# A later order on TensorE in the self-attention loop, and two products that nothing reads behind each of the last five maxima pairs

## The chip, the cores and the metric

One NeuronCore of one Trainium2 chip runs the whole network in one launch. The metric is the device time of that launch in microseconds, as a median of several executions. Five engines work side by side and meet at semaphores: TensorE (PE, with its weight loads shown as PEld), VectorE (DVE), ScalarE (ACT), GpSimd (POOL), and SyncE (SP), which here only issues transfers. Products land in PSUM, eight banks of 128 x 512 fp32.

## The reference

Four layers over x of shape (4, 512, 128), each an attention and a feed-forward part. The change touches the last feed-forward part alone, a transformer block with 16 heads of 8 columns and a mixture of eight experts, of which each token takes one. Cut to what matters:

```
hn = layernorm(x, ln1_g, ln1_b)                      # 4 batches of 512 tokens
q, k, v = hn @ wq + bq, hn @ wk + bk, hn @ wv + bv   # 16 heads of 8
scores = q @ k.T / sqrt(8)                           # 512 x 512 for each head
attn = softmax(scores)                               # with the maximum of each row
x = x + (attn @ v) @ wo + bo
hn2 = layernorm(x, ln2_g, ln2_b)
idx = argmax(hn2 @ gate_w + gate_b)                  # one expert a token
x = x + (relu(hn2 @ w1[idx] + b1[idx]) @ w2[idx] + b2[idx])
```

## The kernel before, in words

`order` (line 2290) writes out the order of all work, and each engine's function runs it once with its own generators, so each engine gets its own instruction stream in one common order. `weave` takes generators with a list of times each (the n-th piece of a generator has the n-th time, or n divided by a number) and always lets the piece with the smallest time go next; on a tie the generator that was given first goes. The times are places in an order and no durations.

**The self-attention loop.** 16 steps, numbered s; a step is one batch (s // 4) and one group of four heads (g = s % 4). Each turn i of the loop (line 2343) works on four steps at once:

- `first(i)`: two pieces of two 128x128 by 128x512 products with selector matrices `SELm` (kept in `RR`, columns 6144 to 8191), which spread queries and keys of four heads over strips of 32 partitions. ScalarE copies them into `QS` and `KS`, which are `QB` and `KB` in a profile.
- `second(i - 1)`: eight pieces, the maxima pairs. TensorE multiplies 32-row queries with 32-row keys into two neighbouring banks (out of banks 0 to 3), and VectorE takes the row maxima of both (line 1825, 128x1024). A ninth piece on TensorE (line 886) transposes the 16 columns of maxima; ScalarE copies them (line 1290), and SyncE sends them by four small transfers (line 2134) into the spare rows of `QS`.
- `third(i - 2)`: waits for these four transfers, then sixteen pieces, one 32-row product each into banks 4, 5 and 6 in turn. The maximum is subtracted inside the product through the spare row. ScalarE follows with an exponential of 128x512 (line 1299). In a profile these products are `PS<-QB,KB`; those of the maxima pairs are `PS<-KB,QB`.
- `fourth(i - 3)`: four pieces of four 128-row products with 32 columns of values each, one for each strip of the array, all into bank 7; fp32 makes two instructions of each, so a piece shows as eight. ScalarE then copies bank 7 to `OT` (line 1307, semaphore `ots`).

Beside them run, in some turns only: `self_norms` (turns 2, 6, 10: the layer norm, values and projections of the next batch; TensorE's transposes are line 837), `tail4` (turns 7, 11, 15: the output of a batch is transposed, normalised and projected, lines 611 and 619), `route3` (turns 8, 12, 16: second layer norm, gate, rank of each token; the sums are line 1855) and `place3` (turn 14). A turn that has none of these is called plain below.

Banks 0 to 3 are given out in pairs where a pair is wanted and singly elsewhere (`Banks.take`, `take_pair`); a bank that was given out waits for its last reader.

Of the kernel before, what the change touches and what calls it, by code (L numbers as in the profile page):

```python
# [164 lines left out]
def program(nc, A, out):  # L165
    with ExitStack() as ctx:
# [292 lines left out]
        def tensor(e, w):  # L459
# [457 lines left out]
            def route3(b):  # L917
# [20 lines left out]
                yield from idle(6)  # L938
# [29 lines left out]
            def place3(g):  # L968
# [4 lines left out]
                yield from idle(14)  # L973
# [73 lines left out]
            order(norm, ahead, front, back, tail, prepare, route, capacity, l2_prepare, self_norms, first, second, third, fourth, tail4,  # L1047
# [3 lines left out]
        def scalar(e, w):  # L1051
# [234 lines left out]
            def second(s):  # L1286
                yield from idle(8)
                w.wait_ge(*mxT.at("s", s))
# [24 lines left out]
            def route3(b):  # L1313
# [5 lines left out]
                yield from idle(10)  # L1319
# [52 lines left out]
            order(norm, ahead, front, back, tail, prepare, route, capacity, l2_prepare, self_norms, first, second, third, fourth, tail4,  # L1372
# [3 lines left out]
        def vector(e, w):  # L1376
# [441 lines left out]
            def second(s):  # L1818
                w.wait_ge(*(mxT.at("s", s - 2) if s >= 2 else scored.at(23, 3, 3)))
                for t in range(4):  # L1820
                    for p2 in range(2):
# [4 lines left out]
                        yield  # L1826
                yield
# [10 lines left out]
            def route3(b):  # L1838
# [19 lines left out]
                yield  # L1858
# [145 lines left out]
            order(norm, ahead, front, back, tail, prepare, route, capacity, l2_prepare, self_norms, first, second, third, fourth, tail4,  # L2004
# [3 lines left out]
        def gpsimd(e, w):  # L2008
# [59 lines left out]
            def route3(b):  # L2068
                yield from layernorm(2, ("r3", b))
                yield from idle(13)  # L2070
# [36 lines left out]
            order(norm, nothing, nothing, nothing, nothing, nothing, route, nothing, nothing, self_norms, nothing, nothing, nothing, nothing, tail4,  # L2107
# [3 lines left out]
        def sync(e, w):  # L2111
# [18 lines left out]
            def second(s):  # L2130
                yield from idle(8)
# [128 lines left out]
            order(nothing, nothing, front, nothing, nothing, nothing, nothing, capacity, nothing, nothing, nothing, second, nothing, nothing,  # L2260
# [29 lines left out]
        def order(norm, ahead, front, back, tail, prepare, route, capacity, l2_prepare, self_norms, first, second, third, fourth, tail4,  # L2290
# [52 lines left out]
            for i in range(19):  # L2343
# [16 lines left out]
                if i in (8, 12, 16):  # L2360
                    streams.append((route3((i - 8) // 4), 26))
# [129 lines left out]
```

## Time and profile before

| what | us |
|---|---|
| median of the runs (3) | 1321.78 |
| lowest and highest | 1306.33, 1324.37 |
| the profiled execution: its own time | 1307.19 |
| its span, first to last instruction | 1305.4 |
| of the span: from the first to the last transpose of maxima | 834.3 to 1171.1 |
| mean granted TensorE clock, whole span | 0.818 of full speed |

The span is one execution. PE busy counts time in which any product is under way, whatever its height. PEclk is the clock that TensorE was granted: 0.50 stands for 1.2 GHz and 1.00 for 2.4 GHz all through a stretch, and a value between them is a mix of both. "Idle before" names what released an engine after it had waited.

### The profile page before, as it was taken

Reading aid. Unit: us, or ns where it says so; the run is one execution under the profiler, and the core shown is the slowest. Engines: PE = TensorE matmul, PEld = TensorE weight load, DVE = VectorE, ACT = ScalarE, POOL = GpSimd, SP = SyncE. Lnnn points to the kernel's source line nnn. Section 1 sums busy time; section 2 is a strip of 40 time slices with the busy share of each in tenths; the row PEclk is TensorE's granted clock in tenths of the full one; section 3 lists DMA queues with packets and bytes.
Section 4 is the critical chain, followed back from the end, with each engine's and each line's share of the span. In section 5 each row is a group of like instructions: output and inputs, shape, how many; then the busy total and the mean of one; then the engine's idle time right before and its main releaser. Section 6 shows DMA issues by size and latency. Waiting matters only on the chain.

```text
span 1305.4 us, 14785 instructions
## 1 busy us (share of the span) xinstructions
PE 1063.3 (81%) x5560; PEld 567.7 (43%) x5560; DVE 635.1 (49%) x1651; ACT 438.3 (34%) x842; POOL 139.6 (11%) x136
## 2 busy tenths in 40 slices
PE   4788999999976773866988887699888889778984
PEld 2344576665523432653653333333333343334653
DVE  4345656555544442337434434755564554652532
ACT  2334333232232220112313233255454454444431
POOL 1000000000011012025211001100100100200222
PEclk7789999999987775986889789676686875768987
DMA  9500000000210001121010000000000000001122
GB/s 294 162 1 1 1 1 1 1 1 1 88 42 4 4 6 35 41 56 21 2 38 1 1 1 1 1 1 1 1 1 1 1 1 1 17 1 31 41 62 71
DMA packets 31359, 33.73 MB, mean 26 GB/s; under 512 B 4053, under 2 KB 22893, under 8 KB 31160
## 3 DMA queue, kind: packets, MB, share of 16 engines
q1 hardware_dynamic: 29240, 28.99, 7.2%
q0 software_dynamic: 2048, 3.79, 1.1%
q8 instruction: 45, 0.74, 0.2%
q14 instruction: 26, 0.21, 0.1%
HBM read 23.31 MB, written 9.70 MB: 25 GB/s over the span
## 4 chain that ended last, share of the span: by engine, by line
PE 70%; DVE 18%; issue 5%; ACT 4%; POOL 2%; DMA 1%; SPq 0%; POOLq 0%; DVEq 0%; ACTq 0%
PE PS L177 63%; DVE KB L1825 4%; DVE KB L1494 3%; PE PS L611 3%; DVE Ht L1396 1%; POOL OT L2030 1%; DVE OT L1535 1%; PE PS L1005 1%; DVE st L1383 1%; POOL ve L2013 1%; DVE CX L1535 1%; PE PS L619 1%; PE PS L521 1%; ACT CX L1299 1%; ACT PT L1177 0%
## 5 line engine op out<-in xcount | busy, mean ns | idle before, releaser
L1825 DVE TENSOR_REDUCE KB<-PS 128x2 fp32r<-128x1024 f32 x128 | 153.6, 1222 | 125.6 <-PE PS L177 125.5
L1177 ACT ACTIVATE PT<-PS 77x512 f32<-77x512 f32 x192 | 98.2, 591 | 158.7 <-PE PS L177 158.7
L177 PE MATMUL PS<-CX 32*77 32x512 f32 (+2 forms) x896 | 128.2, 582 | 18.6 <-DVE OT L1535 7.6
L177 PE MATMUL PS<-HT,RA 128*128 128x512 f32 x288 | 132.0, 601 | 0.0
L2013 POOL TENSOR_TENSOR ve<-ve,nh 128x4 f32<-128x4 f32 x40 | 41.5, 1037 | 694.4 <-DVE ve L1391 694.4
L177 PE MATMUL PS<-QB,KB 32*128 32x512 f32 x256 | 108.4, 616 | 5.7 <-ACT PT L1299 2.3
L177 PEld LDWEIGHTS PS<-RA,PT 128*128 128x128 f32 x816 | 98.9, 193 | 16.3 <-issue 16.3
L177 PE MATMUL PS<-RA,PT 128*128 128x128 f32 (+1 forms) x816 | 102.9, 277 | 1.7 <-DVE PT L1942 1.3
L1494 DVE TENSOR_REDUCE KB<-PS 128x16 fp32r<-128x1232 f32 x48 | 69.1, 1440 | 71.0 <-PE PS L177 70.7
L177 PE MATMUL PS<-KB,QB 32*128 32x512 f32 x256 | 89.7, 598 | 10.8 <-DVE KB L1825 4.7
L1211 ACT ACTIVATE PT<-PS 128x512 f32<-128x512 f32 x72 | 43.0, 597 | 127.2 <-PE PS L177 127.2
L1662 DVE TENSOR_TENSOR PT<-PT,PS 128x512 f32<-128x512 f32 x72 | 49.5, 688 | 57.3 <-PE PS L177 48.0
L177 PEld LDWEIGHTS PS<-CX 32*128 32x128 f32 (+1 forms) x896 | 48.1, 193 | 66.9 <-issue 22.7
L177 PEld LDWEIGHTS PS<-HT,RA 128*128 128x128 f32 x288 | 52.4, 192 | 54.1 <-issue 53.2
L1299 ACT ACTIVATE PT<-PS 128x512 f32<-128x512 f32 x112 | 60.4, 615 | 38.8 <-PE PS L177 38.7
L177 PEld LDWEIGHTS PS<-QB,KB 32*128 32x128 f32 x256 | 45.6, 229 | 62.4 <-issue 23.4
L177 PE MATMUL PS<-PT,VB 77*32 77x512 f32 x384 | 56.5, 664 | 7.7 <-DVE KB L1494 3.5
L177 PEld LDWEIGHTS PS<-KB,QB 32*128 32x128 f32 x256 | 34.8, 233 | 51.6 <-issue 28.5
L177 PE MATMUL PS<-PT,RB 128*32 128x512 f32 x224 | 56.8, 854 | 0.0
L177 PE MATMUL PS<-HT,S 128*128 128x512 f32 x56 | 43.1, 871 | 15.1 <-DVE KB L1494 10.9
L1299 ACT ACTIVATE CX<-PS 128x512 f32<-128x512 f32 x78 | 42.4, 609 | 32.0 <-PE PS L177 32.0
L177 PE MATMUL PS<-RB,PT 128*128 128x128 f32 (+2 forms) x352 | 49.7, 302 | 3.9 <-DVE PT L1519 3.1
(260 smaller groups left out, 1568.2 us busy)
## 6 DMA issues: line engine op xcount, KB each, us to landing
RA<-in_l_w SPq DMA_DIRECT2D x1, 2304.0 KB, 11.1
RB<-in_l_w SPq DMA_DIRECT2D x1, 2048.0 KB, 14.2
RA<-in_l_w SPq DMA_DIRECT2D x1, 2048.0 KB, 8.6
d<-OT SPq DMA_DIRECT2D x2, 960.0 KB, 7.9
RB<-d SPq DMA_DIRECT2D x6, 256.0 KB, 2.9
o<-PT SPq DMA_DIRECT2D x6, 256.0 KB, 2.3
dbuf<-OT SPq DMA_DIRECT2D x2, 640.0 KB, 4.7
X<-in_x SPq DMA_DIRECT2D x4, 256.0 KB, 4.7
```

The source lines that it names most:

```text
L177: return e.matmul(o, l, r, start=first, stop=last, skip_group_check=True)
L521: m = e.transpose(PS[:, 1, 128 * t:128 * t + 128], Hv[i % 2][:, 128 * t:128 * t + 128], ident[:, :])
L611: m = e.transpose(PS[:, k, 128 * hg:128 * hg + 128], outputs_at(key, hg)[:, 128 * j:128 * j + 128], ident[:, :])
L619: m = e.transpose(PS[:, k, 128 * j:128 * j + 128], ON[:, 256 * j + 128 * c:256 * j + 128 * c + 128], ident[:, :])
L1177: e.activation(slot[s][0:NK, :], PS[0:NK, 4 + j, :], ACT.Exp, bias=0.0, scale=a.scale).then_inc(*expd(i, r, j))
L1211: e.activation(slot[s], PS[:, banks.of(silu, i, x, c), :], ACT.Silu).then_inc(*silu(i, x, c))
L1299: e.activation(exps[p], PS[:, banks.of(expd, "s", s, c, j), :], ACT.Exp, bias=0.0, scale=a4.scale).then_inc(*expd("s", s, c, j))
L1494: e.tensor_reduce(o, PS[:, 0:4, 0:308].rearrange("p i (r k) -> p i r k", k=NK), AX, ALU.max).then_inc(*rmax(i, t))
L1535: e.tensor_copy(outputs_at((i,), r), PS[:, 0, :]).then_inc(*otc(i, r))
L1662: e.tensor_tensor(P, P, PS[:, banks.of(glu, i, x, c), :], ALU.mult).then_inc(*glu(i, x, c))
L1825: e.tensor_reduce(o, PS[:, k:k + 2, :], AX, ALU.max).then_inc(*rmax("s", s, t, p2))
L2013: e.tensor_tensor(ve[:, 8 * par + 4:8 * par + 8], ve[:, 8 * par:8 * par + 4], nh[:, :], ALU.pow).then_inc(*rstd(*key))
```

## The change

- The ninth piece of `second` becomes a generator `maxima` of its own. It ran at 0.86 of turn s + 1 and now runs at 0.07 of turn s + 2, between the second and third piece of values; `third` of the same step starts at 0.25 of that turn, where it started at 0.2, and its pieces stand closer together (0.046 for 0.05). The pairs of `second` stand 0.122 apart for 0.11.
- ScalarE's copy of bank 7 goes from 0.5 to 0.3.
- The pieces of `tail4`, `self_norms` and `route3` get times of their own: in `self_norms` the second normalisation goes from 0.467 to 0.4 and TensorE's transposes of it from 0.533 to 0.55; in `route3` the transposes go from 0.154 to 0.32, the gate's product from 0.23 to 0.45, the ranks from 0.5 to 0.78, the last product from 0.615 to 0.92.
- From step 2 on, behind each of the last five maxima pairs of a step, TensorE waits for `ots` of step s - 2 and issues two 128x128 by 128x512 products of selectors into bank 7, which nothing reads: ten in a step, 140 in all.

```diff
                         m.then_inc(*raw("s", s, t, p2))
+                        if s >= 2 and (t, p2) > (1, 0):
+                            w.wait_ge(*ots.at("s", (s - 2) // 4, (s - 2) % 4))
+                            for _ in range(2):
+                                mm(e, PS[:, 7, :], SELm[:, 0, 0, :], RR[:, 6144:6656])
                         yield
+
+            def maxima(s):
                 k, free = banks.take(mts, "s", s)
                 w.wait_ge(*free)
                 w.wait_ge(*rmax.at("s", s, 3, 1))
...
-                    streams.append((second(i - 1), [0.01 + 0.11 * n for n in range(8)] + [0.86]))
+                    streams.append((second(i - 1), [0.01 + 0.122 * n for n in range(8)]))
                 if 2 <= i <= 17:
-                    streams.append((third(i - 2), [0.2 + 0.05 * n for n in range(16)]))
+                    streams.append((maxima(i - 2), [0.07]))
+                    streams.append((third(i - 2), [0.25 + 0.046 * n for n in range(16)]))
                 if i >= 3:
-                    streams.append((fourth(i - 3), [0.0, 0.06, 0.12, 0.18, 0.5]))
+                    streams.append((fourth(i - 3), [0.0, 0.06, 0.12, 0.18, 0.3]))
...
                 if i >= 7 and g == 3:
-                    streams.append((tail4((i - 7) // 4), 14, 0.1))
+                    streams.append((tail4((i - 7) // 4), [0.1, 0.16, 0.22, 0.28, 0.43, 0.57, 0.7]))
                 if g == 2 and b < 3:
-                    streams.append((self_norms(b + 1), 15))
+                    streams.append((self_norms(b + 1), [0.02, 0.1, 0.12, 0.2, 0.22, 0.3, 0.32, 0.4, 0.55, 0.56, 0.67, 0.75, 0.83]))
                 if i in (8, 12, 16):
-                    streams.append((route3((i - 8) // 4), 26))
+                    streams.append((route3((i - 8) // 4), [0.02, 0.1, 0.12, 0.2, 0.32, 0.33, 0.45, 0.46, 0.49, 0.51, 0.53, 0.56, 0.59,
+                                                           0.62, 0.78, 0.79, 0.8, 0.92, 0.95]))
```

The other engines' generators of `route3` get one or two more empty pieces, so that the ranks and what follows keep their places against TensorE's, and `place3` holds its bank for three pieces instead of giving it back at once.

## Rows read from the trace of the kernel before

**Rows 1.** The page: span, engines' busy time, clock in 40 slices, chain that ended last.

```profile
span 1305.4 us, 14785 instructions
PE 1063.3 (81%) x5560; PEld 567.7 (43%) x5560; DVE 635.1 (49%) x1651; ACT 438.3 (34%) x842; POOL 139.6 (11%) x136
...
PEclk7789999999987775986889789676686875768987
...
PE 70%; DVE 18%; issue 5%; ACT 4%; POOL 2%; DMA 1%; SPq 0%; POOLq 0%; DVEq 0%; ACTq 0%
```

**Rows 2.** Busy time by stretch: the self-attention loop, and what follows it.

```profile
core 0: us, PE busy (x) PEld busy (x) DVE busy (x) ACT busy (x) POOL busy (x), PEclk, DMA share, GB/s
834.30:1171.10 336.80, 285.24 (x1216) 115.74 (x1216) 189.94 (x338) 163.64 (x313) 24.77 (x23) 0.69 0.01 3
...
1190.00:1305.00 115.00, 84.58 (x512) 62.75 (x508) 44.49 (x140) 34.95 (x88) 26.19 (x26) 0.89 0.18 53
```

**Rows 3.** Busy time by stretch, single turns: values and scores, by turns.

```profile
893.40:904.10 10.70, 10.70 (x42) 2.55 (x40) 2.45 (x2) 2.37 (x4) 0.00 (x0) 0.50 0.00 1
904.10:913.90 9.80, 8.51 (x37) 4.17 (x37) 7.83 (x10) 7.74 (x16) 0.00 (x0) 0.67 0.01 2
857.60:863.60 6.00, 6.00 (x42) 1.69 (x40) 2.45 (x2) 2.37 (x5) 0.00 (x0) 1.00 0.01 1
...
951.50:962.50 11.00, 9.28 (x47) 5.24 (x46) 9.29 (x15) 8.27 (x16) 1.27 (x1) 0.86 0.00 0
962.50:972.80 10.30, 10.30 (x46) 2.82 (x46) 4.27 (x13) 3.41 (x6) 1.02 (x1) 0.65 0.00 1
972.80:989.00 16.20, 11.88 (x57) 7.14 (x53) 9.48 (x18) 8.47 (x17) 0.00 (x0) 0.61 0.01 2
884.30:887.70 3.40, 2.96 (x16) 1.27 (x12) 2.80 (x3) 3.03 (x7) 0.00 (x0) 0.99 0.00 0
887.70:891.10 3.40, 3.40 (x13) 2.12 (x10) 3.16 (x4) 3.40 (x9) 0.00 (x0) 0.51 0.00 0
```

**Rows 4.** Timeline of TensorE, plain turn: start us, us, instructions [idle before <-releaser].

```profile
892.35 0.37 PE L886 MATMUL PS<-ident,KB 128*16 128x128 f32 x1 [0.85 <-DVE KB L1825]
892.66 0.79 PE L177 MATMUL PS<-QB,KB 32*128 32x512 f32 x2
893.38 1.94 PE L177 MATMUL PS<-CX,RB 128*32 128x512 f32 x8
895.24 0.79 PE L177 MATMUL PS<-KB,QB 32*128 32x512 f32 x2
895.97 1.22 PE L177 MATMUL PS<-QB,RR 128*128 128x512 f32 x2
897.12 1.07 PE L177 MATMUL PS<-CX,RB 128*32 128x512 f32 x2
```

**Rows 5.** The same view where the clock is at its upper level.

```profile
859.08 0.73 PE L177 MATMUL PS<-STG,RR 128*128 128x512 f32 x2
859.74 1.06 PE L177 MATMUL PS<-PT,RB 128*32 128x512 f32 x8
860.74 0.73 PE L177 MATMUL PS<-KN,RR 128*128 128x512 f32 x2
861.40 0.50 PE L177 MATMUL PS<-KB,QB 32*128 32x512 f32 x2
861.84 0.62 PE L177 MATMUL PS<-MT,RB 128*32 128x512 f32 x1
...
863.69 0.50 PE L177 MATMUL PS<-QB,KB 32*128 32x512 f32 x1
...
864.03 0.39 PE L177 MATMUL PS<-QB,KB 32*128 32x512 f32 x1
```

**Rows 6.** Timeline of ScalarE in a scores stretch.

```profile
884.67 3.04 ACT L1299 ACTIVATE CX<-PS 128x512 f32<-128x512 f32 x6 [4.18 <-PE PS L177]
...
888.03 0.67 ACT L1307 ACTIVATE OT<-PS 128x512 f32<-128x512 f32 x1
```

**Rows 7.** Line 886, the transposes of maxima: what TensorE waited for (us, times).

```profile
  DVE KB L1825: 38.1, 29
```

**Rows 8.** Line 837, the transposes of `self_norms`: the same.

```profile
  DVE Ht L1396: 10.9, 3
```

**Rows 9.** Timeline of TensorE in a turn with `route3`.

```profile
979.47 0.61 PE L177 MATMUL PS<-rt,tri 128*128 128x32 f32 x2 [2.05 <-DVE CT L1855]
...
981.28 0.79 PE L177 MATMUL PS<-QB,KB 32*128 32x512 f32 x1
...
981.88 0.62 PE L177 MATMUL PS<-KB,QB 32*128 32x512 f32 x1
983.27 1.40 PE L177 MATMUL PS<-b2t,S 8*128 8x128 f32 x5 [0.77 <-issue]
...
986.10 1.21 PE L177 MATMUL PS<-QB,KB 32*128 32x512 f32 x2
```

**Rows 10.** Timeline of ScalarE's copy and SyncE's issues; then stretches with the transfers.

```profile
892.76 0.27 ACT L1290 ACTIVATE KB<-PS 16x128 fp32r<-16x128 f32 x1 [0.63 <-PE PS L886]
...
893.06 2.42 SPq L2134 DMA_DIRECT2D QB<-KB  x4
...
896.00:897.00 1.00, 1.00 (x4) 0.46 (x2) 0.85 (x1) 0.00 (x0) 0.00 (x0) 0.50 0.01 2
897.00:898.00 1.00, 1.00 (x9) 0.20 (x8) 0.37 (x1) 0.60 (x1) 0.00 (x0) 0.50 0.00 0
```

More of the change, by code:

```diff
@@ L937, in route3 @@
                 banks.free(k)
-                yield from idle(6)
+                yield from idle(7)
                 R = rt[:, 512 * (b % 2):512 * (b % 2) + 512]
@@ L972, in place3 @@
                 mm(e, PS[:, k, 0:8], ones[:, :], P3[g][:, 64:72]).then_inc(*e3("count", g))
-                yield from idle(14)
+                banks.hold(k)
+                yield from idle(2)
+                banks.free(k)
+                yield from idle(12)
             def experts3(g):
@@ L1045, in gather3 @@
                 return none()
-            order(norm, ahead, front, back, tail, prepare, route, capacity, l2_prepare, self_norms, first, second, third, fourth, tail4,
+            order(norm, ahead, front, back, tail, prepare, route, capacity, l2_prepare, self_norms, first, second, maxima, third, fourth, tail4,
                   route3, place3, experts3, gather3, hook)
@@ L1287, in second, with maxima @@
                 yield from idle(8)
+            def maxima(s):
                 w.wait_ge(*mxT.at("s", s))
@@ L1318, in route3 @@
                 e.activation(slot[9], PS[:, banks.of(a3e, b, "T"), :], ACT.Identity, bias=cols[:, 28:29], scale=cols[:, 27:28]).then_inc(*a3e(b, "T"))
-                yield from idle(10)
+                yield from idle(11)
                 w.wait_ge(*e3.at("w", b))
@@ L1370, in gather3 @@
                 return none()
-            order(norm, ahead, front, back, tail, prepare, route, capacity, l2_prepare, self_norms, first, second, third, fourth, tail4,
+            order(norm, ahead, front, back, tail, prepare, route, capacity, l2_prepare, self_norms, first, second, maxima, third, fourth, tail4,
                   route3, place3, experts3, gather3, lambda *a: None)
@@ L1826, in second, with maxima @@
                         yield
+            def maxima(s):
                 yield
@@ L1857, in route3 @@
                 route_.also(*key, "sums")
-                yield
+                yield from idle(2)
                 w.wait_ge(*e3.at("rank", b))
@@ L2003, in vector @@
             m.then_inc(*init("sel"))
-            order(norm, ahead, front, back, tail, prepare, route, capacity, l2_prepare, self_norms, first, second, third, fourth, tail4,
+            order(norm, ahead, front, back, tail, prepare, route, capacity, l2_prepare, self_norms, first, second, maxima, third, fourth, tail4,
                   route3, place3, experts3, gather3, hook)
@@ L2069, in route3 @@
                 yield from layernorm(2, ("r3", b))
-                yield from idle(13)
+                yield from idle(14)
             def place3(g):
@@ L2106, in gpsimd @@
             e.memset(prev[:, 0:8], 0.0).then_inc(*pinit("prev"))
-            order(norm, nothing, nothing, nothing, nothing, nothing, route, nothing, nothing, self_norms, nothing, nothing, nothing, nothing, tail4,
+            order(norm, nothing, nothing, nothing, nothing, nothing, route, nothing, nothing, self_norms, nothing, nothing, nothing, nothing, nothing, tail4,
                   route3, place3, nothing, gather3, hook)
@@ L2128, in front, with maxima @@
                     yield from idle(GATE)
-            def second(s):
-                yield from idle(8)
+            def maxima(s):
                 w.wait_ge(*mts.at("s", s))
@@ L2259, in sync @@
                 load("zero3", d3[i].rearrange("(p t) d -> p (t d)", p=128), OT[:, 0:128 * NT])
-            order(nothing, nothing, front, nothing, nothing, nothing, nothing, capacity, nothing, nothing, nothing, second, nothing, nothing,
+            order(nothing, nothing, front, nothing, nothing, nothing, nothing, capacity, nothing, nothing, nothing, nothing, maxima, nothing, nothing,
                   nothing, nothing, nothing, experts3, gather3, hook)
@@ L2288, in expert_steps, with order @@
                     yield from down(i - 2)
-        def order(norm, ahead, front, back, tail, prepare, route, capacity, l2_prepare, self_norms, first, second, third, fourth, tail4,
+        def order(norm, ahead, front, back, tail, prepare, route, capacity, l2_prepare, self_norms, first, second, maxima, third, fourth, tail4,
                   route3, place3, experts3, gather3, hook):
```

## The prediction

> **What bounds the kernel now.** I read the page first [rows 1]: TensorE is busy for 81% of the span and 70% of the chain that ended last runs through it, and the clock slices from the 26th on stand mostly at 6 to 8 tenths. Then the busy times by stretch [rows 2]: the loop that is changed takes 336.8 of 1305.4 us, with PE busy 285 of them at a granted clock of 0.69; behind it 115 us run at 0.89 and are not touched but for a few empty pieces. Only the 337 us are at stake.
>
> A plain turn has two halves [rows 3]. Its **values stretch** (893.4 to 904.1, values and selector products, all 128 rows tall) has TensorE busy for 10.70 of 10.70 us at 1.2 GHz; the same instructions (x42) take 6.00 us at 2.4 GHz (857.6 to 863.6). Its **scores stretch** (904.1 to 913.9) holds 32-row products and is not TensorE's: ScalarE does six exponentials in 3.04 us [rows 6], 0.49 each with the overlap, 7.8 for sixteen; the rest is the wait for the last maxima [rows 4]. The clock is granted the wrong way round: 0.99 in 884.3 to 887.7, where the scores don't need it, and 0.51 in the 3.4 us behind, in which TensorE was busy for 3.40 [rows 3]. So it fell while 32-row products alone filled the engine, and rose behind stretches of 128-row ones (tall ones, below). That is what the added products aim at.
>
> What the trace says of busy time is worth holding against a page. The Trainium skill (TensorE: Matmul & The Clock Gate, Why this matters for your kernels) asks for TensorE kept busy without idle gaps between bursts, and the full clock should then last. By that rule this stretch was at the full clock already, the added products have nothing to lift and are only paid for, and the time would be that of the slower rival below, 1356. The trace does not agree: busy for 3.40 of 3.40 us, and the clock is at 0.51 [rows 3].
>
> **Part by part**, against the profiled execution's 1307.19 us.
>
> (a) *The wait before the transpose of maxima goes.* TensorE stands before line 886 until the last reduction is done; its two queues wait 38.1 us in 29 waits for it [rows 7], about 19 us each, 1.2 a step. In the new order four pieces (about 4 us) lie between the last pair and the transpose. I take 1.2 x 14 = -17.
>
> (b) *The transpose now stands inside the values stretch*: 0.37 us at the lower clock [rows 4], in some 11 turns: +4. Its cover gets thin. From the start of the transpose (892.35) over copy and four issues (893.06 to 895.5) to the last traffic (before 897) [rows 4, 10] pass about 4.6 us; `third`, with pairs queued behind it, waits for that. Behind the transpose now stand one selector piece, two value pieces and a pair: 1.15 + 2 x 1.86 + 0.73 = 5.6 us at 1.2 GHz [rows 4], enough, but 0.37 + 0.66 + 2 x about 0.9 + 0.44 = 3.3 at 2.4 GHz [rows 5], 1.3 short. SyncE's queue holds nothing else there; ScalarE's copy stands between two selector copies and delays nothing.
>
> (c) *`self_norms`.* The transposes of line 837 wait 10.9 us in 3 for the second normalisation [rows 8]. It comes one maxima pair earlier and TensorE's piece a bit later, with six score pieces and two dummy pairs between: -3.6 x 3 = -11.
>
> (d) *`route3`.* The scores stretch of such a turn takes 16.2 us where a plain one takes 9.8 [rows 3]; printed gaps are 2.05 and 0.77 [rows 9], and ScalarE has to start again behind each. With the pieces spread I take -4 a turn: -12.
>
> (e) *The ten added products.* Price of two: 1.15 us at 1.2 GHz (895.97 to 897.12) [rows 4] and 0.66 at 2.4 (859.08 to 859.74) [rows 5], since a 128-row weight load is not hidden behind a 128-row product. The first waits for `ots`: first exponential 0.67 behind the first score product (884.0, by 884.67) [rows 6], two of 0.49, copy 0.67: 2.35 us, with three scores and two pairs under it; what is queued behind is the fourth score, so ScalarE runs dry for about half a microsecond. Then one block for each pair: two dummies, 2.65 scores, a pair. The five 32-row products need two rounds of the four strips, 0.59 apart at 1.2 GHz (981.28 to 981.88) [rows 9] and 0.34 at 2.4 (863.69 to 864.03) [rows 5], then 0.72 (892.66 to 893.38) or 0.43 to the next tall one: 1.15 + 0.59 + 0.72 = 2.46 us cold, 0.66 + 0.34 + 0.43 = 1.43 warm. ScalarE needs 2.65 x 0.49 = 1.30. Warm, the dummies are nearly free; cold, TensorE becomes the bound. The whole stretch cold: 2.35 + 4 x 2.46 + 1.15 + 0.72 = 14.1 us against 9.8 - 1.2 = 8.6 now: +5.5; warm: 2.35 + 4 x 1.43 + 0.66 + 0.34 = 9.1.
>
> Which clock? In the about 2.3 us before the first dummy there are seven 32-row products and idle time, and where the values ran warm the 1.3 us of (b) come before. That is just the company in which the clock fell before [rows 3], so I expect plain scores stretches to start warm at best and to run cold from there; a rise inside them I don't expect: tall products would take 1.15 of the 2.46 us of a cold block, and the rise in the rows came behind a stretch that they filled. Of the +5.5 I give 0.9 back for the part that is still warm: +4.6 x 6 plain turns = +28. In the five turns with `self_norms` or `route3` (6, 8, 10, 12, 16) some dummies fill places where TensorE idled: +3 x 5 = +15. In the three `tail4` turns, where transposes 128 rows tall fill the gap (0.86 in 951.5 to 962.5 already [rows 3]), they run warm: +1 x 3.
>
> (f) *The clock carried on.* In a `tail4` turn the clock now lasts through the scores (-1.5 x 3 of the 11.0), and the next turn's values stretch starts warm: 10.3 [rows 3] becomes 6.0 + 1.3 of waiting, -3 x 3. Together -13.5.
>
> Sum: -17 + 4 - 11 - 12 + 28 + 15 + 3 - 13.5 = -3.5, so 1303.7 us for an execution like the profiled one. The three runs and the profiled one have a mean of 1314.9, 7.7 above it; I carry that over: 1311, rounded to **1310**. The remaining edits (a bank held longer, empty pieces, the order of arguments) are 0: they fall on banks and engines that have slack there. Unknown prices and ends: (e) from +9 (1 us in 9 steps, the warm price) to +77 (5.5 x 14), (a), (c) and (d) from 0 to -50 together.
>
> **Rivals.**
>
> *The clock holds.* Should the tall products keep 2.4 GHz through every scores stretch, a plain turn is 7.3 + 9.1 = 16.4 instead of 20.5: -25 for six. The five mixed turns, some 27 us each now, lose their waits and halve their values stretch: about -7.5 each, -37. Tail turns -6, turn 2 -4: -72, **1243**. For it: the clock stands at 0.86 in 951.5 to 962.5, where tall products stand among the scores [rows 3]. Against it: 2.3 to 3.6 us nearly without them come in each turn before the first dummy, and nothing in the change shortens that.
>
> *The order wins, the products cost little.* If the clock rises in the middle of the scores stretches, or scores and dummies pack tighter than one behind another, (e) is about +15 instead of +46: -34.5, **1280**. For it: the waits of (a), (c), (d) are in the rows, the packing is only my estimate.
>
> *Slower: dummies cold in every turn.* The place is the wait for `ots` at the first dummy pair; it decides from the point where the clock falls in `tail4` turns as well. Then (e) is 5.5 x 14 = +77 and (f) is 0: -17 + 4 - 11 - 12 + 77 = +41, **1356** with the 7.7. The page's rule, by which the added products change no clock, ends here too.
>
> *The later order does nothing*, because what it moves becomes late again (the transfers of (b), the pairs behind them): (a), (c), (d) are 0 and the rest stays, +36.5: **1352**.
>
> **Chances.** Forecast 0.42, order wins 0.22, clock holds 0.12, cold everywhere 0.16, order does nothing 0.05, 0.03 for the rest. The range 1262 to 1352 leaves out the clock that holds and half of the cold rival. About 2% (26 us) is what a measurement of this kernel can tell from no change; against 1321.78 faster means under 1295. That is 0.12 + most of the 0.22 + an edge of the forecast = 0.35; slower, over 1348: 0.17; within: 0.48.
>
> **What would show it.** (a) no wait on line 1825 left before line 886. (b) in a warm values stretch a gap of about 1.3 us before the first `PS<-QB,KB`. (c), (d) lines 837 and 1855 without waits of over 1 us. (e) clock near 0.5 in plain scores stretches of about 13 us, with `PS<-RR` pairs 1.15 long. (f) a clock over 0.9 in `tail4` turns and in the values stretch behind. I am wrong if plain scores stretches show a clock above 0.8: then the total is under 1285. I am wrong the other way if turns 7, 11 and 15 get longer.

## The result: slower by 3%, outside the range

| what | before | after |
|---|---|---|
| median of four runs, us | 1318.75 | 1360.12 |
| lowest and highest, us | 1306.33, 1324.37 | 1344.73, 1364.34 |
| the profiled execution and its span, us | 1307.19, 1305.4 | 1344.73, 1342.8 |
| ratio of the times, 95% interval | | 1.0306 [1.0192, 1.0419] |

The median is 50 us above the 1310 of the prediction and 8 us above the upper end of its range; the lower end of the interval is 1.9%. Of the rivals the slower one (1356) comes nearest. Ratios here and below leave disturbed executions out, while medians take in all, so a ratio is not the quotient of two medians.

The page after, the lines that answer to [rows 1], and the row of the added products, which the page of before doesn't have:

```profile
span 1342.8 us, 15039 instructions
...
PE 1117.4 (83%) x5700; PEld 589.6 (44%) x5700; DVE 638.1 (48%) x1651; ACT 442.8 (33%) x842; POOL 139.5 (10%) x136
...
PEclk7899999999987757968978986677666766767987
...
PE 72%; DVE 14%; ACT 4%; issue 4%; DMA 2%; POOL 2%; SPq 1%; POOLq 0%; DVEq 0%; ACTq 0%
...
L177 PE MATMUL PS<-RR 128*128 128x512 f32 x140 | 75.3, 633 | 10.6 <-ACT OT L1319 10.6
```

TensorE is busy for 54 us more, the span is 37 longer, and VectorE went from 18% of the chain to 14%: waits for VectorE were exchanged for work of TensorE. To place it, take the stretch from the first value product of turn 3 to the last one of the loop. Busy times by stretch (columns as in [rows 2]), this one, before and then after:

```profile
857.70:1190.20 332.50, 285.95 (x1247) 112.99 (x1246) 173.89 (x298) 162.15 (x312) 21.47 (x20) 0.70 0.01 4
```

```profile
850.10:1228.20 378.10, 346.91 (x1388) 140.98 (x1386) 178.39 (x299) 167.15 (x313) 21.40 (x20) 0.68 0.01 4
```

The loop is 45.6 us longer (the first 850 us were 7.6 shorter in this execution, the end is the same). PE busy grew by 61.0: more than the whole loss. Cut at each turn's first value product and first score product (worked out from the start times, as all lengths of stretches below that no line shows), the values stretches sum to 140.7 us (142.3 before) and the scores stretches to 237.5 (190.2 before): the loss is in the scores. "Warm" and "cold" below stand for the upper and the lower level of the granted clock, "tall" for products of 128 rows. The same view of single stretches after, in the order values of turn 5, first 2.1 us of its scores, the rest of them; values and scores (in three pieces) of turn 7, a `tail4` turn; scores of turn 8, a `route3` turn:

```profile
893.40:901.40 8.00, 7.07 (x43) 1.65 (x41) 2.45 (x2) 2.64 (x5) 0.00 (x0) 0.89 0.00 1
901.40:903.50 2.10, 0.84 (x7) 0.41 (x7) 1.31 (x2) 1.55 (x4) 0.00 (x0) 1.00 0.00 0
903.50:913.60 10.10, 10.03 (x32) 4.46 (x32) 5.95 (x5) 6.32 (x13) 0.00 (x0) 0.59 0.01 2
...
941.30:949.10 7.80, 7.80 (x55) 2.94 (x53) 3.73 (x7) 2.64 (x5) 0.00 (x0) 1.00 0.00 1
949.10:953.00 3.90, 3.00 (x15) 1.56 (x14) 2.94 (x6) 2.18 (x4) 0.00 (x0) 1.00 0.00 0
953.00:957.00 4.00, 4.00 (x11) 1.82 (x11) 1.54 (x2) 2.28 (x4) 0.00 (x0) 0.52 0.00 0
957.00:967.80 10.80, 10.74 (x31) 5.42 (x30) 4.58 (x5) 4.34 (x8) 1.26 (x1) 0.50 0.00 0
...
977.60:998.20 20.60, 19.61 (x70) 11.04 (x70) 9.52 (x19) 9.94 (x18) 0.00 (x0) 0.57 0.00 0
```

Read the clock column downwards. In the plain turn it is at its upper level up to the first added pair and then mostly at the lower one, with TensorE busy for 10.03 of 10.10 us. In the `tail4` turn too, which was at 0.86 over its scores before [rows 3]. The `route3` turn has TensorE busy for 19.6 of 20.6 us; before it was 11.88 of 16.2 [rows 3].

The timeline of TensorE after, in the scores stretch of turn 5 (start us, us, instructions, idle before):

```profile
901.42 0.49 PE L177 MATMUL PS<-QB,KB 32*128 32x512 f32 x1 [0.94 <-DMA QB<-KB]
...
903.58 0.73 PE L177 MATMUL PS<-RR 128*128 128x512 f32 x2 [1.32 <-ACT OT L1319]
904.24 0.50 PE L177 MATMUL PS<-QB,KB 32*128 32x512 f32 x3
...
904.91 0.86 PE L177 MATMUL PS<-RR 128*128 128x512 f32 x2
907.12 1.22 PE L177 MATMUL PS<-RR 128*128 128x512 f32 x2
908.28 0.79 PE L177 MATMUL PS<-QB,KB 32*128 32x512 f32 x2
...
909.42 1.22 PE L177 MATMUL PS<-RR 128*128 128x512 f32 x2
...
911.73 1.22 PE L177 MATMUL PS<-RR 128*128 128x512 f32 x2
```

Two idle pieces stand in front of the tall products: 0.94 us for the transfers and 1.32 for `ots`. The first pair still takes 0.73, the third 1.22, and from there one block follows another at 2.30 and 2.31 us.

### The profile page after: what moved, and what is told of

It is laid out like the page before. It is cut to its first block, busy times and chain, and to the rows that moved or that the text cites. A ratio compares the mean times of both kernels' runs of the same rounds, so it can differ in the third digit from the quotient of the medians.

```text
span 1342.8 us, 15039 instructions
## 1 busy us (share of the span) xinstructions
PE 1117.4 (83%) x5700; PEld 589.6 (44%) x5700; DVE 638.1 (48%) x1651; ACT 442.8 (33%) x842; POOL 139.5 (10%) x136
## 4 chain that ended last, share of the span: by engine, by line
PE 72%; DVE 14%; ACT 4%; issue 4%; DMA 2%; POOL 2%; SPq 1%; POOLq 0%; DVEq 0%; ACTq 0%
PE PS L177 65%; DVE KB L1506 3%; PE PS L611 2%; DVE KB L1837 2%; SPq L2147 1%; DMA QB<-KB 1%; POOL OT L2044 1%; DVE Ht L1408 1%; DVE OT L1547 1%; PE PS L1015 1%; DVE st L1395 1%; PE PS L619 1%; POOL ve L2027 1%; DVE CX L1547 1%; PE PS L521 1%
## 5 line engine op out<-in xcount | busy, mean ns | idle before, releaser
L177 PE MATMUL PS<-QB,KB 32*128 32x512 f32 x256 | 98.2, 674 | 11.6 <-DMA QB<-KB 10.5
L177 PE MATMUL PS<-RR 128*128 128x512 f32 x140 | 75.3, 633 | 10.6 <-ACT OT L1319 10.6
L177 PEld LDWEIGHTS PS<-QB,KB 32*128 32x128 f32 x256 | 38.5, 244 | 79.6 <-DMA QB<-KB 21.0
L177 PE MATMUL PS<-HT,S 128*128 128x512 f32 x56 | 42.5, 859 | 15.4 <-DVE KB L1506 10.9
```

Of the source, the lines that this page charges most:

```text
L177: return e.matmul(o, l, r, start=first, stop=last, skip_group_check=True)
```

## Experiments

The theory before the runs: the added products are paid at the lower clock because two idle pieces and 32-row products lie ahead of the first one. Rivals: the products cost what they cost at any clock; or the later order is what lost.

Times of all, each against the kernel before beside it on the same chip:

| kernel | median, us | ratio [95%] |
|---|---|---|
| `a_order_only` | 1298.11 | 0.9831 [0.9747, 0.9916] |
| `b_wait_only` | 1309.33 | 0.9913 [0.9873, 0.9954] |
| `c_products_old_order` | 1369.12 | 1.0355 [1.0249, 1.0460] |
| `d_one_product` | 1344.02 | 1.0175 [1.0087, 1.0264] |
| `e_short_products` | 1322.56 | 1.0067 [1.0013, 1.0122] |
| `f_filled` | 1323.40 | 0.9990 [0.9944, 1.0036] |
| `g_filled_early_maxima` | 1317.50 | 0.9976 [0.9931, 1.0021] |
| `h_order_early_maxima` | 1300.23 | 0.9840 [0.9760, 0.9920] |
| `i_no_route_turns` | 1301.26 | 0.9893 [0.9851, 0.9935] |
| `j_no_tail_route_turns` | 1291.54 | 0.9824 [0.9741, 0.9907] |
| the same again, `j2_...` | 1303.41 | 0.9873 [0.9827, 0.9920] |
| `k_filled_one_product` | 1342.37 | 1.0206 [1.0139, 1.0272] |
| `l_maxima_moved_only` | 1325.33 | 1.0097 [1.0056, 1.0137] |
| `n_plain_turns_only` | 1295.33 | 0.9802 [0.9756, 0.9848] |
| `a2_order_only` | 1298.73 | 0.9846 [0.9797, 0.9895] |
| `q_early_copy` | 1315.41 | 0.9956 [0.9917, 0.9994] |
| `p_fill_no_pairs` | 1314.56 | 0.9975 [0.9932, 1.0017] |

`a`, `b`, `c`, `d` ran on one chip, `e` to `h` on a second, `i` to `l` on a third, `n`, `j2`, `a2`, `q` on a fourth, `p` and the change itself each by themselves. Between such groups half a percent is not to be read: for `e` the quotient of the medians is 0.9993 where the ratio is 1.0067.

### The parts of the change: order, wait, products

`a_order_only` drops the wait and the products; `b_wait_only` keeps the wait; `d_one_product` has one product for two.

```diff
                         m.then_inc(*raw("s", s, t, p2))
-                        if s >= 2 and (t, p2) > (1, 0):
-
-                            w.wait_ge(*ots.at("s", (s - 2) // 4, (s - 2) % 4))
-                            for _ in range(2):                 # d: range(1)
-                                mm(e, PS[:, 7, :], SELm[:, 0, 0, :], RR[:, 6144:6656])
                         yield
```

> The changed kernel without the added products and without their wait for the copy of bank 7: the later order alone. Theory (the added products are paid in TensorE's own time at 1.2 GHz, and they also eat the waits that the order removes): terms (a) to (d) of the prediction show at last, -17 + 4 - 11 - 12 = -36 us, ratio to the kernel before about 0.973, scores stretches of turns 7 and 11 (with tail4) near 12 us, of turns 8 and 12 (with route3) near 11 to 12. Rival (the later order is at fault: the short way of the maxima and the pieces moved back are late again): ratio 1.01 or more, route3 turns stay near 20 us of scores.

> The changed kernel with the wait for the copy of bank 7 behind the fourth maxima pair, but without the products. Theory (the products' time is the price): half a microsecond a turn over the order alone, +7 us in 14 turns, ratio about 0.978. Rival (the wait is the price, about 2.3 us from the first score product, in 14 turns): +30 us over the order alone, ratio 1.0 or more.

> The changed kernel with one product behind each of the last five pairs instead of two, 70 fewer in all. Theory: each product at 1.2 GHz costs about 0.575 us of TensorE's time, 5 fewer a turn make 2.9 us, in 14 turns -40 us against the changed kernel, ratio to the kernel before about 1.00, clocks as before the change. Rival (the products hardly cost, order or wait does): less than -12 us, ratio over 1.02.

`c_products_old_order` is the kernel before with the wait and the two products put in, and ScalarE's copy at 0.3 for 0.5.

> The kernel before with the wait and the ten products a step, all pieces at their old places but ScalarE's copy of bank 7, which goes to 0.3 (at 0.5 the wait could not be met). Theory: 14 turns x 4 to 5.5 us of products at 1.2 GHz over the kernel before, less what falls in its waits for norms and routing (about 20 us), so +35 to +55 us, ratio 1.03 to 1.04. Rival (order at fault): +10 to +20, ratio about 1.01.

The order alone is faster than before by 1.7% (expected was 2.7%), and `a2_order_only` below says the same. Differences of ratios, at 1320 us: the wait costs 0.0082 or 11 us (expected 7), the first 70 products 0.0262 or 35 us, the second 70 0.0131 or 17 us. The intervals of `a` and `b` overlap, and so do those of `d` and the change, but the loops of the traces stand in the same order: 317.6, 331.2, 371.9 and 378.1 us. All products and the wait together cost 63 us on the new order and 47 us on the old one (expected 35 to 55). So the rival "the order lost" falls. For `d` a gain of 40 us over the changed kernel was expected and 17 came: the first product behind a pair costs more than the second. The first 70 cost 0.5 us each and the second 70 0.25, where a product takes 0.58 us at 1.2 GHz and 0.33 at 2.4 [rows 4, 5]; the times alone don't say at which clock they were paid. The busy times of `a_order_only`, the loop, scores of a plain turn, scores of turn 8 (`route3`):

```profile
859.60:1177.20 317.60, 284.08 (x1248) 115.54 (x1247) 176.64 (x299) 161.67 (x313) 21.39 (x20) 0.70 0.01 4
887.40:895.70 8.30, 7.52 (x33) 3.67 (x29) 7.23 (x7) 7.75 (x16) 0.00 (x0) 0.81 0.00 0
966.10:980.30 14.20, 11.72 (x60) 7.47 (x61) 9.35 (x19) 9.62 (x18) 0.00 (x0) 0.67 0.01 1
```

The order takes 14.9 us out of the loop with nearly the same PE busy (284.1 for 285.2 in [rows 2] and 286.0 in the stretch above). In the plain turn ScalarE is now busy for 7.75 of 8.30 us, the bound named in the prediction; in the `route3` turn 2.5 us of waits are left for ten added products to fill, which at the lower clock take 5.8.

### Short products

`e_short_products` gives the added products 32 rows for 128 (`SELm[0:32, ...]`, `RR[0:32, ...]`), all else as in the change.

> The changed kernel with the 140 added products 32 rows tall instead of 128: same count, columns, bank and wait. Theory (their price is that a product over all four strips can run beside nothing, and holds up the 32-row products around it): they now run beside scores and pairs, and the time comes down to near the kernel with the wait alone, ratio 0.99 to 1.00, clock in scores stretches 0.6 to 0.7. Rival (the price is issue and streaming of 140 more products, whatever their height): as the changed kernel, ratio 1.03.

Against the changed kernel the ratio falls from 1.0306 to 1.0067, some 32 us. Stretches of it, plain scores and `tail4` scores:

```profile
887.00:896.40 9.40, 8.07 (x38) 5.60 (x38) 7.16 (x6) 8.05 (x16) 0.00 (x0) 0.67 0.00 0
951.80:966.10 14.30, 13.35 (x55) 8.20 (x54) 8.81 (x11) 9.04 (x17) 1.27 (x1) 0.61 0.00 0
```

The scores of plain turns are within 0.2 us of before, cut in the same way (in turn 9 they are 0.6 longer). About half of the 63 us hangs on the height of the products; of the rest 11 us are the wait, and 20 stay with products of 32 rows, where the theory had next to nothing. The clock in the `tail4` turn is low here as well (0.61, TensorE busy for 13.35 of 14.30 us), so it takes no tall products to lose it there.

### Closing the gap in front of the first product

`f_filled` moves ScalarE's copy from 0.3 to 0.19 (right behind the values; the first pieces of `tail4` to 0.1, 0.13, 0.15, 0.17, ahead of it), puts three products in front of a step's scores, behind the wait for `ots` of step s - 1, and lets pair products begin one pair earlier. `g` has the maxima at 0.05 for 0.07 besides, and `h` is `a_order_only` with 0.05.

```diff
-                        if s >= 2 and (t, p2) > (1, 0):
+                        if s >= 2 and (t, p2) > (0, 1):
...
+                if s >= 1:
+                    w.wait_ge(*ots.at("s", (s - 1) // 4, (s - 1) % 4))
+                    for _ in range(3):
+                        mm(e, PS[:, 7, :], SELm[:, 0, 0, :], RR[:, 6144:6656])
                 w.wait_ge(*mq[s % 2].at("s", s))
...
-                    streams.append((fourth(i - 3), [0.0, 0.06, 0.12, 0.18, 0.3]))
+                    streams.append((fourth(i - 3), [0.0, 0.06, 0.12, 0.18, 0.19]))
```

`f` and `g` issue 213 added products, 168 behind pairs and 45 in front of scores; where the expectation has another count, this one holds.

> The changed kernel with the low places filled: ScalarE copies bank 7 at 0.19, ahead of the exponentials; three products stand ahead of the first score piece, where TensorE waits for the transfers of the maxima, and two more behind the third pair, so that products start with the scores; the first four pieces of tail4 stand closer (0.1 to 0.17). 215 more tall products than the change has would be 28 + 45 = 73; in all 213. Theory (the clock was lost in the gap between the values and the first product, and would have held otherwise): granted clock over 0.9 in the scores stretches, plain turns of 16 to 18 us, ratio 0.95 to 0.98. Rival (two products a pair never hold the clock, gap or not): clock 0.6, plain turns of 24 us, ratio 1.05 or more.

> As the filled kernel, with the transpose of maxima at 0.05, one value piece earlier, so that the transfers land before they are waited for even at 2.4 GHz. Theory (clock holds, the way of the maxima bounds the start of the scores): 0.5 us a turn less than the filled kernel, -7 us. Rival (it does not hold): no difference.

> The later order alone, without products or their wait, and with the transpose of maxima at 0.05. Theory (in the order alone the values stretches that run at 2.4 GHz end up to 1.5 us before the maxima have landed): -0.5 us in about half of the turns, -4 us against the order alone, ratio 0.98. Rival (the transpose now waits for the last reduction, as before the change): +5 to +15 us.

With 73 products more than the changed kernel, `g` is some 44 us faster (1.0306 to 0.9976). `f` and `g` kept the clock in plain turns, as expected, and yet are no faster than the kernel before, where 0.95 to 0.98 was expected. Values and scores of turn 4 in `g`, and its scores in turn 12 (`route3`):

```profile
880.20:888.20 8.00, 7.28 (x47) 2.21 (x46) 2.51 (x3) 3.02 (x7) 0.00 (x0) 1.00 0.00 1
888.20:897.40 9.20, 9.20 (x41) 4.20 (x40) 7.25 (x6) 7.43 (x15) 0.00 (x0) 1.00 0.00 0
...
1067.20:1088.00 20.80, 20.36 (x73) 11.33 (x76) 9.16 (x17) 9.66 (x17) 0.00 (x0) 0.59 0.00 1
```

The clock stays at 1.00 through a whole plain turn of 17.2 us, TensorE busy for all of the scores. It does so although one idle piece is left, 0.72 us in front of the three products, where they wait for ScalarE's copy:

```profile
887.26 0.96 PE L177 MATMUL PS<-RR 128*128 128x512 f32 x3 [0.72 <-ACT OT L1323]
```

This is the rival "the clock holds" (7.3 + 9.1 = 16.4 by the prediction), reached with another kernel. In turn 12 it falls, and the scores are as long as after the change (20.8 and 20.6 us). `h` against `a_order_only`, and `g` against `f`, show nothing that stands clear of the noise: moving the maxima by one piece is no cause.

### One cause at a time: the copy alone, fillers alone, one product

`q_early_copy` is the changed kernel with ScalarE's copy at 0.19 for 0.3 and the first four pieces of `tail4` moved ahead of it as in `f_filled`, nothing else. In turns without `tail4` it changes the copy alone; in turns 7, 11 and 15 it changes two things at once.

> The changed kernel with its ten products a step, and only ScalarE's copy of bank 7 at 0.19 (the first pieces of tail4 at 0.1 to 0.17, which the copy waits for): no product ahead of the scores, none behind the third pair. Theory (each part of the low place between the values and the first product costs the clock; without the copy's 2.3 us the 1.5 us of waiting for the transfers and the pieces without products behind it are left): clock in plain scores stretches between 0.7 and 0.9, plain turns of 19 to 21 us, ratio 1.01 to 1.02. Rival (the late copy alone lost the clock): clock 1.0, plain turns of 17 us, ratio 1.00 or less.

It is 1315.41 us: the ratio goes from 1.0306 to 0.9956, some 46 us, with the same 140 products. The theory had 1.01 to 1.02; the rival, that the late copy alone lost the clock, comes nearer. Its timeline of TensorE in the scores of turn 4, and the start of those of turn 5:

```profile
889.51 0.49 PE L177 MATMUL PS<-QB,KB 32*128 32x512 f32 x1
...
890.33 0.74 PE L177 MATMUL PS<-RR 128*128 128x512 f32 x2
...
893.74 0.73 PE L177 MATMUL PS<-RR 128*128 128x512 f32 x2
...
895.18 0.73 PE L177 MATMUL PS<-RR 128*128 128x512 f32 x2
...
896.65 0.73 PE L177 MATMUL PS<-RR 128*128 128x512 f32 x2
...
905.14 0.49 PE L177 MATMUL PS<-QB,KB 32*128 32x512 f32 x1 [0.94 <-DMA QB<-KB]
...
910.01 1.22 PE L177 MATMUL PS<-RR 128*128 128x512 f32 x2
```

And the busy times: values of turn 5, scores of turn 5, and scores of turn 9.

```profile
897.90:905.10 7.20, 6.29 (x42) 1.60 (x41) 2.56 (x3) 3.18 (x7) 0.00 (x0) 1.00 0.01 1
...
905.10:916.50 11.40, 11.36 (x41) 4.95 (x42) 7.17 (x6) 7.28 (x14) 0.00 (x0) 0.64 0.01 1
```

```profile
981.90:990.20 8.30, 8.30 (x33) 4.65 (x31) 2.98 (x5) 3.95 (x7) 0.00 (x0) 0.50 0.00 0
1000.00:1008.40 8.40, 8.39 (x42) 4.02 (x45) 7.13 (x6) 7.33 (x16) 0.00 (x0) 1.00 0.01 2
```

In turn 4 no idle time stands in front of the first pair, the clock lasts, and blocks follow each other at 1.44 and 1.47 us (the prediction's warm block was 1.43). A warm turn 4 then makes a warm values stretch in turn 5, 7.2 us; that is too short for the transfers, 0.94 us of idle time appears in front of the scores, and the clock falls in them. Turns 4, 9 and 13 are of the first kind (scores 8.3 to 8.4 us), 3 and 5 of the second (11.4 and 11.7). The `tail4` turns stay warm through their scores, which take 11.4 us in each where they took 18.7 to 19.0 after the change. Turn 7:

```profile
953.30:964.70 11.40, 10.69 (x57) 5.51 (x53) 8.20 (x8) 8.47 (x17) 1.27 (x1) 1.00 0.00 0
```

Of the 42.6 us by which the loop of `q` is shorter than that of the changed kernel, the six plain turns (14 with them) give 18 and the `tail4` turns 13; another 8 come from the `route3` turns, most of it from their values. So less than half of the gain is shown to be the copy's alone; which of the two edits kept `tail4` turns warm was not tested.

The first row of the fence with scores of turn 9 is the second half of a `route3` turn's scores, all at the lower level: the early copy doesn't save these.

`p_fill_no_pairs` is `g` with only the 45 products in front of the scores; `k_filled_one_product` is `g` with one product behind a pair.

> The filled kernel with the early transpose, without any product behind the pairs; the three ahead of the scores, 45 in all, and the early copy stay. Theory (products have to stand among the scores for the clock to last through them): clock in plain scores stretches 0.6 to 0.8 again, their length 8.3 us, plain turns about 18.5, ratio 0.98 to 0.985. Rival (the three products ahead of the scores hold the clock alone): clock over 0.9 and plain turns of 16 us, ratio 0.97 or less.

> The filled kernel with the early transpose, with one product behind a pair instead of two. Theory (it takes enough tall work all the way to hold the clock): one is too few, clock in plain scores stretches falls to 0.6 to 0.8, plain turns of 18.5 to 20 us against 17.2. Rival (filling the gap is all that counts): clock 1.0, plain turns 16.5 us, ratio 0.98.

Scores of a plain turn in `p`, then in `k`:

```profile
887.40:895.20 7.80, 7.36 (x30) 4.08 (x29) 6.68 (x6) 7.27 (x15) 0.00 (x0) 0.63 0.00 0
```

```profile
895.10:905.80 10.70, 10.70 (x35) 4.51 (x34) 7.26 (x6) 7.49 (x14) 0.00 (x0) 0.65 0.00 0
```

Without products among the scores the clock falls there (0.63 over the stretch), though three products stand in front. With one behind each pair it falls as well, and with TensorE busy for 10.70 of 10.70 us. Of the kernels tried only those with two behind each pair and no late copy hold it through the scores of plain turns (`q` in three of five). Among the filled kernels one product is the worst number (1.0206, against 0.9975 with none and 0.9976 with two): paid at the lower clock, and buying nothing. Both expectations had the clock right and the time too low (`p` 0.98 to 0.985).

### Where products stand in vain

`i_no_route_turns` is `g` without pair products in steps 7, 11, 15 (turns 8, 12, 16); `j` without those of steps 6, 10, 14 (turns 7, 11, 15) too; `n_plain_turns_only` is `j` besides without the three ahead of the scores for steps 5, 6, 9, 10, 13, 14. `j2` is `j` again, beside `a2`, the order alone again. The edit of `j` and `n`, the second part in `n` alone:

```diff
-                        if s >= 2 and (t, p2) > (0, 1):
+                        if s >= 2 and s not in (6, 7, 10, 11, 14, 15) and (t, p2) > (0, 1):
...
-                if s >= 1:
+                if s >= 1 and s not in (5, 6, 9, 10, 13, 14):
```

> The filled kernel with the early transpose, without the products behind the pairs in turns 8, 12 and 16 (steps 7, 11, 15), where the filled kernel ran its scores at 1.2 GHz. Theory (products pay where they hold the clock and cost their full time where they don't): these turns come down from 26 to 28.7 us to about 23, all others stay, -12 to -15 us against that kernel, ratio 0.985 to 0.99, level with the order alone. Rival (without them the clock falls in the turns behind as well): plain turns 9 and 13 lose 2 us or more, no gain.

> The same, without products behind the pairs in turns 7, 11 and 15 either. Theory (tail turns run at 2.4 GHz with the products and pay them fully there, since TensorE is the bound): 2 us less in each of the three, -6 us against the kernel with the products left out in route turns. Rival (they hold the clock for what follows): turns 7, 11, 15 go to a clock of 0.7 and 1 to 3 us longer, and the values of turns 8, 12, 16 slow down.

> The kernel without products behind the pairs in tail4 and route3 turns, also without the three ahead of the scores there. Theory (there they cost their time and hold no clock that lasts): 1 to 1.5 us less in each of six turns, -6 us against the kernel that keeps them, ratio 0.978. Rival (they shorten the low place for the values behind): no gain or +3 us.

> The kernel without products behind the pairs in tail4 and route3 turns once more, beside the order alone on the same chip. Theory (products held where they hold the clock are worth a little): 0.982 to the kernel before, 0 to 8 us below the order alone. Rival (no product is worth its time): level with the order alone or above.

> The later order alone once more, for the comparison on one chip: 0.983 to the kernel before by either theory.

Leaving them out of the `route3` turns shortens the scores of turn 8 from 18.1 to 13.8 us and the whole from 0.9976 to 0.9893. `n` is at 0.9802, 3.4 us below `a2` on the same chip, and their intervals overlap by more than half of each. `j` and `j2` are one kernel on two chips, 1291.54 and 1303.41 us or 0.9824 and 0.9873 of the kernel before: so far apart can two measurements of one kernel be. `j2` is 4.7 us above `a2`, where its theory had it below. So the best kernel with products and the order without any can't be told apart: both beat the kernel before and the changed one, and no use of the products is shown to be worth having over none. In `n` the plain turns 4 and 5 take 17.3 us at 1.00 (values 7.28 of 8.00 busy, scores 9.30 of 9.30), while `a_order_only` takes 18.1 and 17.1 there at 0.59 to 0.81. The higher clock bought next to nothing there, since warm scores with products in them (9.3) are longer than cold ones without (8.3).

### The order in two parts

`l_maxima_moved_only` is `a_order_only` with `tail4`, `self_norms` and `route3` at their old times and pieces.

> The kernel before with the transpose of maxima moved into the next turn and the times of the pairs, scores and copy of bank 7 that go with it; tail4, self_norms and route3 at their old places; no products. Theory (terms (a) and (b) of the prediction): plain turns of 18 us as in the order alone, turns with norms and routes 2 to 4 us longer than there, ratio 0.99. Rival (the whole gain of the later order is the maxima): ratio 0.98 to 0.985, as the order alone.

At 1.0097 it is slower than before, where `a_order_only` is 1.7% faster and 0.99 or less was expected; the loop of its trace, too, is 11 us longer than before (343.4 us). Plain turns are as short as with the whole order (17.1 to 18.1 us), but its scores in turn 8:

```profile
973.20:991.40 18.20, 10.29 (x48) 5.79 (x47) 9.03 (x18) 8.75 (x17) 0.00 (x0) 0.60 0.00 1
```

TensorE is idle for 7.9 of 18.2 us. The maxima's move makes `route3` and `self_norms` turns wait more (scores 20.0 and 20.5 us in turns 6 and 10, 18.0 before), and the times written out for them take that back and more. So the prediction's term (a), priced as a gain by itself, is a loss when its edit stands alone. The other part alone was not run.

## Why the prediction was wrong

The sum is set beside the loop in the traces, 45.6 us longer where the terms gave -3.5, with `a_order_only` as the middle point: -14.9 from before to the order alone, +60.5 from there to after. Of the 49 us between forecast and measurement 21 lie in the order's gain, 19 in (e) and 9 in (f).

**(a), (c), (d), with (b): -36 predicted, -14.9 measured in the traces, -22 by the ratio.** The waits went, as said. After the change the transposes of maxima (now line 893) wait for no engine where it was 38.1 us [rows 7], and line 837 waits for 3.0 where it was 10.9 [rows 8] (us, times, for the one and the other line). What is printed for line 893 stands in the weight-load queue alone, so half of the 38.1, TensorE's own, is what went:

```profile
  issue: 20.0, 15
```

```profile
  DVE Ht L1408: 3.0, 2
```

With the order alone the values stretches sum to 145.5 us (142.3 before), +3.2 for (b)'s +4; single turns moved by -2.2 to +3.7 us with the clock they met, so the agreement of the sum is partly luck. The scores sum to 172.1 (190.2), -18.1 where (a), (c) and (d) said -40. A wait removed shortened a plain scores stretch by 0.9 to 1.1 us, down to ScalarE's sixteen exponentials, so (a) was near right there; the two `self_norms` turns of the stretch gave 2.1 and -0.5 us for the 3.6 and 1.2 each; the `route3` turns 2.2 to 2.5 for 4 and 1.2; the `tail4` turns 0.1 to 0.9 for 1.2. (c) and (d) are the terms that were too large: I had priced each of their waits at its full length.

**(e): +46 predicted, +65.4 measured** (scores 172.1 to 237.5), by kinds of turn:

| turns | predicted | measured, order alone to after |
|---|---|---|
| plain, and 14 (six) | +28 | +21 |
| mixed 6, 8, 10, 12, 16 | +15 | +23 |
| `tail4` 7, 11, 15 | +3 | +21 |

For plain turns the block of 2.46 us was 2.30, the mechanism as written (turn 14, at a clock of 0.94, paid only 1.2 us). **The step that failed is the price for the other turns** (+18 forecast, +44 measured), "some dummies fill places where TensorE idled" and "they run warm". For `route3` it needed one addition: PE busy of 11.9 in 16.2 us [rows 3], ten products at 0.58 make 17.7 against a stretch that (d) had just shortened to 12. The removed waits and the added products are on one engine, and I counted the same idle time as a gain in (d) and as cover in (e). Measured: scores 14.2 us with the order alone, 20.6 after. The addition still falls 2.9 short; TensorE was busy for 19.6 us, and how much of the rest is the lower clock (0.67 to 0.57) and how much 32-row products that no longer run beside each other was not separated. In `tail4` turns the transposes fill some of the gap, as I said, but the clock falls, from 953 on, 4 us behind the start of the scores; the slower rival had put the deciding point there, at the wait for `ots`. The order already brings it down from 0.86, as this stretch of `a_order_only` shows (turn 7, scores), and the products then stand at the lower level:

```profile
945.60:957.30 11.70, 10.49 (x46) 6.05 (x45) 8.34 (x11) 8.65 (x17) 1.27 (x1) 0.71 0.00 0
```

**(f): -13.5 predicted, -4.8 measured** (values 145.5 to 140.7). In the turns behind `tail4` (8, 12, 16), where the -9 was to come from, the values take 9.8, 9.7 and 7.3 us (9.7, 9.8 and 8.5 before). It hung on `tail4` staying warm, and `q_early_copy` shows what it is worth when they do: there the scores of the `tail4` turns are at 1.00 and take 11.4 us (11.3 to 12.0 with the order alone, where more of the transposes stand in them), and the values behind them take 7.2, 7.2 and 6.6 us, for the 7.3 of the prediction. So these terms failed by the clock that they took for granted, and not by their sizes.

What was right: no wait on the maxima reduction left, the wait for `ots` (the first pair 2.16 us behind the first score, for 2.35), the wait for the transfers in warm values (0.94), and cold blocks in plain turns. The waits of the loop after, by what TensorE's weight loads waited for (total us, times, longest):

```profile
PEld PS L177 <- DMA QB<-KB: 18.8, 11, 2.3
...
PEld PS L177 <- ACT OT L1319: 14.6, 11, 1.8
```

The lost clock was put down to these idle pieces with 32-row products around them; turns 4, 9 and 13 of `q_early_copy` show that moving the late copy keeps it, and `p` and `k` that idle time is only a part of it. The rule of the Trainium skill weighed in the prediction (TensorE: Matmul & The Clock Gate, Why this matters for your kernels) asks for no idle gaps between bursts, and the gaps that it names are longer than any of these. By that rule the gaps of 0.94 and 1.32 us should have cost no clock, and `p` and `k` should have been warm too. But the clock is at 0.59 behind these gaps, and at 0.63 and 0.65 in `p` and `k`: here the measurement decides.

With the sizes measured in the traces the prediction's own sum is 1307.2 + 7.7 - 14.9 + 65.4 - 4.8 = 1360.6, against a median of 1360.12. That it meets it so closely is luck: without the 7.7 the sum is 1352.9, and the profiled execution took 1344.73, 7.6 us of the difference lying ahead of the loop, where nothing was changed. The slower rival's 1356 is near by luck as well, since its gain of the order (-36) and its price of the products (+77) were both too large. The range was too narrow at its upper end because it took in the dear products only together with the full gain of the order.

**Open:** what lets 32-row products take the clock down while TensorE is busy throughout; why `route3` scores are at 0.50 even where products fill them (8.30 of 8.30 us busy in `q`), and what a turn needs to start warm after them. Neither the early `tail4` pieces without the early copy nor the order alone with another arrangement of `route3` was tried.

## What to carry to other kernels

Before an added instruction is priced as "filling idle time", add its duration to the engine's busy time in that stretch and hold the sum against the stretch as the same change's other parts leave it; idle time can be counted once. If filler (products that only keep the engine busy) is meant to keep a clock, look for the idle piece in front of it first, and for who makes it: here one late copy of 0.6 us, with the pieces it waited for, stood for some 46 us. And compare the whole with the version that has no filler at all: here ScalarE's exponentials bounded the cold scores (7.75 of 8.30 us), and no kernel with filler was shown to be faster than the order alone.

## What the runs showed of the hardware beyond expectation

- Scores stretches of 32-row products can run at 1.00 throughout (9.20 of 9.20 us busy in `g`) where two 128-row products stand behind each pair and three in front, with 0.72 us idle ahead of these; with one behind each, and TensorE busy throughout as well, the clock is 0.65 (`k`).
- A higher clock can undo itself by way of transfers: the warm values stretch (7.2 us in `q`) ends before four small transfers land, TensorE idles for 0.94 us, and the next stretch has 0.64.
- Granted clock and time need not go together: over the loop `g` has 0.88 and 337.6 us, `a_order_only` 0.70 and 317.6:

```profile
860.40:1198.00 337.60, 315.84 (x1461) 133.31 (x1459) 178.85 (x299) 167.77 (x313) 21.45 (x20) 0.88 0.01 4
```
